# A four-layer graph network on one core: Elu of two attention layers one tick later, and the third layer's sum split over two ticks

## The chip, the cores and the metric

The kernel runs on one core of one Trainium2 chip. The metric is device time in microseconds. Before the change the median of three runs is 7264.87 us (7262.79 to 7265.74).

## What is computed

50,000 nodes with 256 features each pass four blocks; every block is `x = layernorm(x + block(x))`. Block 1 is a hypergraph convolution, block 2 two graph attention layers, block 3 a graph convolution with batch norm, block 4 two more attention layers. 25,000 edges are sorted by target. The change touches block 2 and the first layer of block 4. One attention layer, cut to what matters:

```python
h = (x @ W).reshape(n, HEADS, HID)
e = leaky_relu(a_s[src] + a_d[dst], 0.2)         # self loops are among the edges
ex = exp(e - segment_max(e, dst)[dst])
alpha = ex / segment_sum(ex, dst)[dst]
out = segment_sum(h[src] * alpha[:, :, None], dst).reshape(n, 256) + b
# block 2: elu(out) after each of its two layers, then x = layernorm(x + out)
# block 4, first layer: relu(layernorm(out) * g + b), then W2
```

## The kernel before, in words

The kernel is a row of phases, each with its own buffers and an end at which all engines meet. `layer_phase` (L2465) runs five of them: `l1` (kind `l1a`, first attention layer of block 2), `l2` (`l1b`, second one, with residual and layernorm), `l3` (`gcn`), and, behind a batch-norm phase, `l5` (`l3a`, first attention layer of block 4) and `l6` (`l3b`). The change acts in l1, l2 and l5.

Nodes are permuted so that 25,088 slots (region 0) can have edges that end in them, and as many (region 1) have none. A tile is 128 partitions by 4 rows (J = 4) of one region, so there are 49 tiles of each region, 98 in all. `ORDER` mixes them by hand: in every 11 ticks there are six tiles of region 0 and five of region 1.

A phase is a loop over ticks. In a tick every engine runs its program for that tick, in its own order, and engines are held together only by semaphores. `L` (L2004 to L2012) gives each stage of a tile its tick: a tile with index u in `ORDER` has stage s in tick u + L[s]. Before the change:

- `load` 6: SP loads the tile's rows into ring buffer `a` (L2092), once the tile that held the buffer before is done with. In l2 and l5 that is waiting for `s_z`, which ACT raises when it has normalized that tile (L2244). `resid` loads the residual rows (L2098), `store` stores the result (L2105 in l2, L2113 in l1 and l5). SP takes them in the order batch store L1691, load, resid, store.
- `pre` 8: for region 0 only. ACT scales two of the four rows by the self loop's share (`own_rows`, L2279, eight instructions, the first thing in ACT's tick). DVE (`sum_up`, L2325) scales the edge sums into `part` (L2345), scales the other two rows (L2349), waits for ACT's rows, and adds (L2354), which raises `s_sum`.
- l1 and l2: in tick 9 ACT takes exp of the tile into one of two buffers `ee` (L2257, the last thing in ACT's tick), and in tick 10 (`body`) DVE makes Elu of it (L2373). In l1 this raises `s_u`; in l2 the residual add (L2383) does, and four row statistics (L2399) follow.
- l5: region 1 has its body in tick 8 (four instructions L2390, then the statistics L2399); for region 0, `sum_up` goes on in the same tick with the bias add (L2364) and the statistics.
- With a norm: variance on DVE per pair of tiles (L2408, L2414) one tick after the body, the power -0.5 on POOL (L2131), the shift on DVE (L2421), the norm on ACT five ticks after the body (L2244). l1 and l5 end with transposes (`turn`, PE L2187), their copy (`zt`, ACT L2227 or L2224), the product (PE L2166), and its eviction (DVE L2434 in l1, ACT L2214 in l5).

`Edges` interleaves the edge work: 25 batches of 8 columns, each with POOL gathers (L1667), logits on DVE (L1824 to L1844), their exp on ACT (L1733), weighting and running sums on DVE (L1865, L1881), a copy on ACT that needs the end of the batch (L1737), and shares (L1897 to L1923). DVE's program of a tick is not one part after another: `take_turns` (L114) takes one instruction from each part in turn, edge parts first, then eviction, shift, variance, body, sum.

ACT's order in a tick is own rows, edge work, eviction, `zt`, norm, exp for Elu. So an edge step that comes at the end of DVE's tick (L1733, L1737) holds the `zt`, norm and exp queued behind it.

The ring of `a` has `last - L["load"] + 2` buffers: 7 in l1, 11 in l2, 9 in l5.

Of the kernel before, what the change touches and what calls it, by code (L numbers as in the profile page):

```python
# [7 lines left out]
ALU = mybir.AluOpType  # L8
# [6 lines left out]
D = 256  # L15
# [110 lines left out]
def spread(ap, k):  # L126
    return ap.unsqueeze(len(ap.shape)).to_broadcast([*ap.shape, k])


def over_columns(row, k):  # L130
    return row.unsqueeze(1).to_broadcast([row.shape[0], k, row.shape[1]])
# [1861 lines left out]
class Nodes:  # L1993


    def __init__(self, nc, S, s, kind, edges, rows, rw, resid=None, weight=None, out=None, heads=4, self_act=0):
# [5 lines left out]
        self.mat = kind in ("l1a", "l3a", "gcn")  # L2002
        pre = self.edges.first - SPOT[0] + (4 if self.gat else 2)
        L = self.L = {"pre": pre, "load": pre - 2}  # L2004
        body = L["body"] = pre + 2 if self.elu else pre
        L["resid"] = max(body - 2, 0)
        if self.norm:
            L["var"], L["norm"] = body + 1, body + 5
        L["turn"] = (L["norm"] if self.norm else body) + 1
        L["zt"], L["prod"], L["evict"], L["store"] = (L["turn"] + k for k in (1, 2, 3, 4))  # L2010
        if not self.mat:
            L["store"] = L["norm"] + 1  # L2012
        last = L["norm"] if self.norm else L["turn"]
        self.ra = last - L["load"] + 2
        self.a = [s.sb(f"a{b}", [P, J, rw]) for b in range(self.ra)]
        self.s_in = s.sems("rows_loaded", self.ra)
        if resid is not None:
# [265 lines left out]
    def vector(self, dve, tick):  # L2283
        parts = []
        if tick == 0:
            self.prepare(dve)
        if self.gcn:
            now = self.tile(tick, "store")
            if now:
                parts.append(self.batch_stats(dve, *now))  # L2290
            now = self.tile(tick, "pre")
            if now and now[1] == 0:
                parts.append(self.add_neighbours(dve, *now))
            return parts
        now = self.tile(tick, "evict") if self.kind == "l1a" else None
        if now:
            parts.append(self.evict(dve, *now))
        if self.norm:
            q = self.pair(tick, "var", 3)
            if q is not None:  # L2300
                parts.append(self.shifts(dve, q))
            q = self.pair(tick, "var")
            if q is not None:
                parts.append(self.variance(dve, q))
        now = self.tile(tick, "body")
        if now and (self.elu or now[1]):
            parts.append(self.body(dve, *now))
        now = self.tile(tick, "pre")
        if now and now[1] == 0:
            parts.append(self.sum_up(dve, *now))  # L2310
        return parts
# [13 lines left out]
    def sum_up(self, dve, u, region, t):  # L2325
        H, lk, e = self.heads, self.sum_lk, self.edges
        hw, b, k0 = D // H, t // 2, t % 2 * J
        sh, a = e.share[b % 2], self.a[u % self.ra]
        run = e.run[b % e.nrun][:, k0:k0 + J, 0:D]
        by_head = lambda x: x.rearrange("p j (h c) -> p j h c", h=H)  # L2330
        dve.wait_ge(e.s_nw, b + 1)
        dve.wait_ge(self.s_in[u % self.ra], self.loaded(u))
        sa = self.self_act
        if H == 1:
            dve.wait_ge(self.s_self, t + 1)
            for j in range(J):
                last = dve.scalar_tensor_tensor(a[:, j, 0:D], run[:, j, :], sh[:, 1, k0 + j, 0:1], a[:, j, 0:D], ALU.mult, ALU.add)  # L2337
                if j < J - 1:
                    yield
            last.then_inc(self.s_sum, 1)  # L2340
        else:
            part = self.part[t % 2]
            if t >= 2:
                dve.wait_ge(self.s_sum, t - 1)
            lk.link(dve.tensor_tensor(by_head(part[:]), by_head(run), spread(sh[:, 1, k0:k0 + J, :], hw), ALU.mult))  # L2345
            yield
            if sa < J:
                own = by_head(a[:, sa:J, 0:D])
                lk.link(dve.tensor_tensor(own, own, spread(sh[:, 0, k0 + sa:k0 + J, :], hw), ALU.mult))  # L2349
                yield  # L2350
            lk.settle(dve)
            if sa:
                dve.wait_ge(self.s_self, t + 1)
            dve.tensor_tensor(a[:, :, 0:D], a[:, :, 0:D], part[:], ALU.add).then_inc(self.s_sum, 1)  # L2354
        if self.elu:
            return
        yield
        dve.wait_ge(self.s_sum, t + 1)
        if self.kind == "l3a":
            other = over_columns(self.S["r_L3_gnn_b1"][:], J)  # L2360
        else:
            dve.wait_ge(self.s_rin[u % self.rr], 16 * (u // self.rr + 1))
            other = self.r[u % self.rr][:, :, 0:D]
        dve.tensor_tensor(a[:, :, 0:D], a[:, :, 0:D], other, ALU.add).then_inc(self.s_u, 1)  # L2364
        yield
        dve.wait_ge(self.s_u, u + 1)
        yield from self.row_stats(dve, u)
# [252 lines left out]
```

## Time and profile before

| | us |
|---|---|
| median of three runs | 7264.87 |
| lowest, highest | 7262.79, 7265.74 |
| the profiled execution's own time | 7259.0 |
| its span | 7257.3 |
| phase l1, from its start to the next phase's | about 2832 to 3552 |
| phase l2 | about 3552 to 4404 |
| phase l5 | about 5533 to 6330 |

The profiled execution is 5.9 us below the median. PE is TensorE (PEld its weight loads), DVE VectorE, ACT ScalarE, POOL GpSimd, SP the engine that issues most transfers (SPq its queue). In a row of the timeline or of a line, the number in brackets is the time that the engine stood idle ahead of the instruction, and what ended it. Times in the timeline count from the start of the span; names of tensors have their phase number left out, so `l_a` is `a` in whichever layer phase runs at that time.

### The profile page before, as it was taken

The page shows a single profiled execution, that of the slowest core. Times are in us where ns is not written, and L with a number is a line of the kernel's source. Part 1 is how long each engine was busy: PE and PEld are TensorE (multiplying, and loading weights), DVE is VectorE, ACT ScalarE, POOL GpSimd, SP SyncE. Part 2 cuts the span into 40 slices and gives each one's busy share as a digit, 9 for nine tenths or more (in the row PEclk, how much of TensorE's full clock was granted, in tenths as well). Part 3 has the DMA queues.
Part 4 walks back from the last instruction along what each step waited for, and adds up shares of the span by engine and source line. Part 5 has one row for each costly group of instructions (what it writes and reads, how often), then busy time and mean ns, then how long its engine had stood idle before and what let it go on. Part 6 is the DMA issues. An engine that isn't in the chain of part 4 may idle for free. (4 is left out here: it accounts for less than half of the span.)

```text
span 7257.3 us, 77301 instructions
## 1 busy us (share of the span) xinstructions
PE 3818.6 (53%) x18205; PEld 3002.3 (41%) x18205; DVE 4910.7 (68%) x15616; ACT 3204.3 (44%) x7082; POOL 3988.0 (55%) x3216
## 2 busy tenths in 40 slices
PE   3578880088866884777400005988884666700000
PEld 1267760077755663555400003547773555600000
DVE  6544555545548875999698886866666888676664
ACT  0023330033324552444255555758884777633333
POOL 4767776667766877342244425621114444178887
PEclk9689995599998997999755557999997888855555
DMA  8745447845448996676577767989995666476665
GB/s 307 273 92 77 77 64 272 328 69 78 77 56 318 350 348 212 234 245 235 186 260 260 249 244 286 380 302 327 334 336 188 215 219 211 163 265 226 226 227 188
DMA packets 646102, 1633.93 MB, mean 225 GB/s; under 512 B 128454, under 2 KB 283878, under 8 KB 630290
## 3 DMA queue, kind: packets, MB, share of 16 engines
q1 hardware_dynamic: 459954, 1234.83, 48.9%
q0 software_dynamic: 185696, 394.18, 20.3%
q8 instruction: 150, 2.46, 0.1%
q14 instruction: 302, 2.47, 0.1%
HBM read 816.50 MB, written 813.62 MB: 225 GB/s over the span
## 5 line engine op out<-in xcount | busy, mean ns | idle before, releaser
L1708 PE MATMUL l_pb<-l_jx,k_ones 128*128 128x128 f32 x26 | 6.1, 399 | 1595.9 <-DVE l_jx L1941 1595.9
L802 POOL DMA_INDIRECT NS<-e_tot,e_idx x392 | 647.9, 1653 | 283.3 <-ACT e_tot L1060 210.8
L2244 ACT ACTIVATE l_z<-l_a,l_nb,l_rs 128x256 f32<-128x256 f32 x1176 | 609.7, 598 | 392.7 <-DMA out_dram<-l_z,k_ids 389.9
L1667 POOL DMA_INDIRECT l_eg<-HBT,k_nsrc x392 | 508.2, 1296 | 384.8 <-DVEq L1886 145.0
L1708 PEld LDWEIGHTS l_pb<-l_jx,k_ones 128*128 128x128 f32 x26 | 5.0, 284 | 1596.6 <-DVE l_jx L1941 1596.6
L936 DVE TENSOR_SCALAR e_eq<-e_pk,z_skey 128x128 f32<-128x128 f32 x588 | 204.1, 347 | 621.7 <-DMA NS<-e_tot,e_idx 590.4
L2131 POOL TENSOR_TENSOR l_rs<-l_ve,k_minus_half 128x8 f32<-128x8 f32 x147 | 259.7, 1767 | 533.9 <-DVE l_ve L2414 241.3
L2166 PE MATMUL l_pm<-k_w_L3b,l_zt 128*128 128x258 f32 x1568 | 406.8, 419 | 218.8 <-ACT l_o L2214 214.5
L2138 POOL DMA_INDIRECT out_dram<-l_z,k_ids x392 | 422.1, 1077 | 119.5 <-issue 109.0
L1203 POOL DMA_INDIRECT XH<-n_o,z_home x392 | 399.7, 1020 | 119.2 <-issue 112.4
L2279 ACT ACTIVATE l_a<-l_a,l_eshare 128x64 f32<-128x64 f32 (+1 forms) x1372 | 378.9, 360 | 186.2 <-DVE l_eshare L1923 144.0
L2166 PE MATMUL l_pm<-k_w_L1b,l_zt 128*128 128x264 f32 x1568 | 400.3, 403 | 113.2 <-DVE l_o L2434 109.0
L1060 ACT ACTIVATE e_tot<-e_pa 128x520 f32<-128x520 f32 x196 | 118.3, 604 | 744.2 <-DMA NS<-e_tot,e_idx 731.9
L2399 DVE BATCH_NORM_STATS2 l_bs<-l_a 128x6 f32<-128x256 f32 x1176 | 444.8, 410 | 2.1
L2166 PEld LDWEIGHTS l_pm<-k_w_L3b,l_zt 128*128 128x128 f32 x1568 | 323.3, 212 | 279.1 <-issue 228.2
L1881 DVE SCALAR_TENSOR_TENSOR l_erun<-l_erun,k_same,l_eg 128x260 f32<-128x260 f32 (+2 forms) x880 | 419.7, 477 | 4.0
L1667 POOL DMA_INDIRECT l_eg<-XH,k_psrc x196 | 242.5, 1237 | 323.0 <-DVEq L1886 262.9
L1227 PE MATMUL n_pm<-z_w_L1a,n_zt 128*128 128x264 f32 x1568 | 399.3, 412 | 12.0 <-DVE n_o L1265 11.4
L1011 PE MATMUL e_po<-z_w_e2n,e_hid 128*128 128x256 f32 x1584 | 379.2, 383 | 19.0 <-DVEq L899 19.0
L1020 PE MATMUL e_pr<-e_zt,z_w_n2e 128*128 128x256 f32 x1584 | 379.3, 383 | 0.4 <-issue 0.3
L1420 POOL TENSOR_TENSOR n_rs<-n_ve,k_minus_half 128x8 f32<-128x8 f32 x49 | 80.2, 1636 | 536.7 <-DVE n_ve L1539 536.7
L2166 PEld LDWEIGHTS l_pm<-k_w_L1b,l_zt 128*128 128x128 f32 x1568 | 293.2, 196 | 194.2 <-DVE l_o L2434 114.4
(384 smaller groups left out, 13063.6 us busy)
## 6 DMA issues: line engine op xcount, KB each, us to landing
NS<-z_zero SPq DMA_DIRECT2D x200, 520.0 KB
HBT<-l_o SPq DMA_DIRECT2D x196, 528.0 KB
l_a<-HBT SPq DMA_DIRECT2D x196, 528.0 KB, 9.2
GSUMS<-l_erun SPq DMA_DIRECT2D x72, 1056.0 KB, 5.0
l_a<-XH SPq DMA_DIRECT2D x98, 528.0 KB
HA<-n_o SPq DMA_DIRECT2D x98, 528.0 KB, 7.9
l_a<-HA SPq DMA_DIRECT2D x98, 528.0 KB
n_r<-NS SPq DMA_DIRECT2D x98, 520.0 KB
```

What stands on the lines that cost most here:

```text
L802: pool.indirect_dma_start(out=nodes, out_offset=bass.IndirectOffsetOnAxis(ap=idx[q % DEEP][:, k:k + 1], axis=0), in_=tot[q % 2][:, k, :], ...
L1011: mm = pe.matmul(po[:, k, :], hid[q % 2][:, i, k * P:(k + 1) * P], w2[:, i, 0:D], start=i == 0, stop=i == KC - 1)
L1020: mm = pe.matmul(pr[:, n, :], w1[:, i, n * P:(n + 1) * P], zt[q % 2][:, i].rearrange("p j n -> p (j n)"), start=i == 0, stop=i == KC - 1)
L1203: pool.indirect_dma_start(out=T["XH"], out_offset=bass.IndirectOffsetOnAxis(ap=S["home32"][:, col:col + 1], axis=0), in_=o[t % RO][:, j, : ...
L1227: last = pe.matmul(pm[h][:, i, 0:RW], zt[t % 2][:, k, h * (J // 2) + i, :], weight[:, k, :], start=k == 0, stop=k == KC - 1)
L1667: pool.indirect_dma_start(out=self.g[b % self.ng][:, k, :], out_offset=None, in_=self.table, in_offset=bass.IndirectOffsetOnAxis(ap=self.i ...
L1881: lk.link(dve.scalar_tensor_tensor(rt[:, k, 0:n], before, S["same"][:, b * BC + k:b * BC + k + 1], g[:, k, 0:n], ALU.mult, ALU.add))
L2138: pool.indirect_dma_start(out=self.out, out_offset=bass.IndirectOffsetOnAxis(ap=S["ids32"][:, col:col + 1], axis=0), in_=self.z[u % self.r ...
L2166: last = pe.matmul(self.pm[h][:, i, 0:self.wc], zt[:, k, h * (J // 2) + i, :], self.weight[:, k, 0:self.wc], start=k == 0, stop=k == KC - 1)
L2244: last = act.activation(z[:, j, 0:D], a[:, j, 0:D], ACT.Identity, bias=self.nb[b][:, col:col + 1], scale=self.rs[b][:, col:col + 1])
L2279: last = act.activation(a[:, j, f], a[:, j, f], ACT.Copy, scale=sh[:, 0, t % 2 * J + j, h:h + 1])
L2399: self.stat_lk.link(dve.bn_stats(bs[:, u % 2 * J + j, :], a[:, j, 0:D]))
```

## The change

Elu (`body`) of l1 and l2 comes in tick 11 instead of 10; all stages that are counted from it follow one tick later (resid, variance, norm, turn, zt, prod, evict, store). The exp on ACT stays in tick 9, and there are still two `ee` buffers, so that the exp of tile u now waits for a body (of tile u - 2) of the same tick, not of the tick before. The ring of `a` grows from 7 to 8 buffers in l1 and stays at 11 in l2, where a tile now holds its buffer one tick longer. In l5 `sum_up` ends after its two multiplications in tick 8, and a new part `join_parts` in tick 9 does the add, the bias add and the statistics; region 1's body moves to tick 9 as well, with all later stages one tick later; the ring grows from 9 to 10. No instruction is added or dropped. Phases l3 and l6 are as before.

```diff
--- before.py
+++ after.py
@@ -2002,16 +2002,20 @@
         self.mat = kind in ("l1a", "l3a", "gcn")
         pre = self.edges.first - SPOT[0] + (4 if self.gat else 2)
         L = self.L = {"pre": pre, "load": pre - 2}
-        body = L["body"] = pre + 2 if self.elu else pre
+        body = L["body"] = pre + 3 if self.elu else pre
+        self.split = kind == "l3a"
+        if self.split:
+            body = L["body"] = L["join"] = pre + 1
         L["resid"] = max(body - 2, 0)
         if self.norm:
-            L["var"], L["norm"] = body + 1, body + 5
+            stats = L.get("join", body)
+            L["var"], L["norm"] = stats + 1, stats + 5
         L["turn"] = (L["norm"] if self.norm else body) + 1
         L["zt"], L["prod"], L["evict"], L["store"] = (L["turn"] + k for k in (1, 2, 3, 4))
         if not self.mat:
             L["store"] = L["norm"] + 1
         last = L["norm"] if self.norm else L["turn"]
-        self.ra = last - L["load"] + 2
+        self.ra = last - L["load"] + (1 if kind == "l1b" else 2)
         self.a = [s.sb(f"a{b}", [P, J, rw]) for b in range(self.ra)]
         self.s_in = s.sems("rows_loaded", self.ra)
         if resid is not None:
@@ -2305,6 +2309,9 @@
         now = self.tile(tick, "body")
         if now and (self.elu or now[1]):
             parts.append(self.body(dve, *now))
+        now = self.tile(tick, "join") if self.split else None
+        if now and now[1] == 0:
+            parts.append(self.join_parts(dve, *now))
         now = self.tile(tick, "pre")
         if now and now[1] == 0:
             parts.append(self.sum_up(dve, *now))
@@ -2348,13 +2355,28 @@
                 own = by_head(a[:, sa:J, 0:D])
                 lk.link(dve.tensor_tensor(own, own, spread(sh[:, 0, k0 + sa:k0 + J, :], hw), ALU.mult))
                 yield
-            lk.settle(dve)
-            if sa:
-                dve.wait_ge(self.s_self, t + 1)
-            dve.tensor_tensor(a[:, :, 0:D], a[:, :, 0:D], part[:], ALU.add).then_inc(self.s_sum, 1)
+            if self.split:
+                return
+            yield from self.add_parts(dve, u, t)
         if self.elu:
             return
         yield
+        yield from self.rest_of_sum(dve, u, t)
+
+    def add_parts(self, dve, u, t):
+        a, lk = self.a[u % self.ra], self.sum_lk
+        lk.settle(dve)
+        if self.self_act:
+            dve.wait_ge(self.s_self, t + 1)
+        dve.tensor_tensor(a[:, :, 0:D], a[:, :, 0:D], self.part[t % 2][:], ALU.add).then_inc(self.s_sum, 1)
+        yield
+
+    def join_parts(self, dve, u, region, t):
+        yield from self.add_parts(dve, u, t)
+        yield from self.rest_of_sum(dve, u, t)
+
+    def rest_of_sum(self, dve, u, t):
+        a = self.a[u % self.ra]
         dve.wait_ge(self.s_sum, t + 1)
         if self.kind == "l3a":
             other = over_columns(self.S["r_L3_gnn_b1"][:], J)
```

## Rows read from the trace of the kernel before

**Rows 1.** The page's first line, whole kernel
```profile
span 7257.3 us, 77301 instructions
```
**Rows 2.** Windows, one row a phase: length; busy us (count) of PE, PEld, DVE, ACT, POOL; PEclk, DMA, GB/s
```profile
2832.00:3555.00 723.00, 491.99 (x2384) 391.64 (x2384) 605.28 (x1259) 317.76 (x788) 245.04 (x199) 0.92 0.67 222
3555.00:4396.00 841.00, 6.77 (x28) 5.99 (x28) 741.00 (x2037) 422.15 (x1080) 365.48 (x245) 0.50 0.71 248
5530.00:6328.00 798.00, 489.84 (x2382) 418.49 (x2382) 650.11 (x1994) 542.15 (x1376) 338.58 (x246) 0.82 0.59 200
```
**Rows 3.** Waits of DVE in phase l1 (total us, times, longest us)
```profile
DVE l_a L2373 <- ACT l_ee L2257: 46.1, 37, 1.7
```
**Rows 4.** Waits of DVE in phase l2
```profile
DVE l_a L2373 <- ACT l_ee L2257: 79.4, 33, 3.0
```
**Rows 5.** Waits of DVE in phase l5
```profile
DVE l_a L2354 <- ACT l_a L2279: 89.8, 24, 5.7
```
**Rows 6.** Windows of the three phases without their first and last stretches
```profile
2890.00:3515.00 625.00, 458.84 (x2215) 363.24 (x2216) 553.50 (x1157) 300.62 (x747) 204.99 (x165) 0.96 0.69 235
3600.00:4345.00 745.00, 5.25 (x22) 4.56 (x22) 664.38 (x1823) 378.98 (x979) 320.28 (x210) 0.50 0.72 251
5600.00:6263.00 663.00, 432.59 (x2074) 368.26 (x2075) 571.68 (x1766) 481.42 (x1233) 279.84 (x200) 0.84 0.62 209
```
**Rows 7.** Waits of DVE in the last 65 us of phase l5
```profile
DVE l_a L2354 <- ACT l_a L2279: 5.7, 1, 5.7
```
**Rows 8.** Timeline of l1, one tick: start us, us, engine, line, operation
```profile
3140.61 2.01 ACT L2279 ACTIVATE l_a<-l_a,l_eshare 128x64 f32<-128x64 f32 x8
3140.76 1.23 DVE L2373 SCALAR_TENSOR_TENSOR l_a<-l_ee,l_a 128x1024 f32<-128x1024 f32 x1 [0.87 <-ACT l_ee L2257]
...
3145.69 1.23 DVE L2354 TENSOR_TENSOR l_a<-l_a,l_part 128x1024 f32<-128x1024 f32 x1
```
**Rows 9.** Timeline of l2, one tick with own rows behind a late end of batch
```profile
3971.20 0.26 ACT L1737 ACTIVATE l_erun<-l_em 128x32 f32<-128x32 f32 x1 [9.70 <-DVEq L1886]
...
3974.95 1.66 POOL L2131 TENSOR_TENSOR l_rs<-l_ve,k_minus_half 128x8 f32<-128x8 f32 x1 [0.69 <-ACT l_z L2244]
...
3975.72 2.00 ACT L2279 ACTIVATE l_a<-l_a,l_eshare 128x64 f32<-128x64 f32 x8
3975.84 1.23 DVE L2373 SCALAR_TENSOR_TENSOR l_a<-l_ee,l_a 128x1024 f32<-128x1024 f32 x1 [3.01 <-ACT l_ee L2257]
...
3980.37 1.21 DVE L2354 TENSOR_TENSOR l_a<-l_a,l_part 128x1024 f32<-128x1024 f32 x1
```
**Rows 10.** Row loads of l2: timeline around one load, and the landing times (line L2092)
```profile
3939.20 0.43 SPq L2092 DMA_DIRECT2D l_a<-HBT  x1
...
3942.15 0.32 SPq L2105 DMA_DIRECT2D X<-l_z  x1
...
3955.96 2.02 ACT L2279 ACTIVATE l_a<-l_a,l_eshare 128x64 f32<-128x64 f32 x8 [3.06 <-DVE l_eshare L1923]
...
DMA to landing us min/median/max: 5.5/9.5/10.1
```
**Rows 11.** Timeline of l5: one add that waits, and the body work of another tile
```profile
5918.47 0.68 DVE L2349 TENSOR_TENSOR l_a<-l_a,l_eshare 128x512 f32<-128x512 f32 x1
...
5921.64 2.02 ACT L2279 ACTIVATE l_a<-l_a,l_eshare 128x64 f32<-128x64 f32 x8
...
5923.76 1.28 DVE L2354 TENSOR_TENSOR l_a<-l_a,l_part 128x1024 f32<-128x1024 f32 x1 [4.61 <-ACT l_a L2279]
...
5926.33 1.41 DVE L2399 BATCH_NORM_STATS2 l_bs<-l_a 128x6 f32<-128x256 f32 x4
...
5928.31 1.64 DVE L2390 SCALAR_TENSOR_TENSOR l_a<-l_a,k_loop,k_r_L_gnn_b 128x256 f32<-128x256 f32 x4
```
**Rows 12.** Timeline of the end of l1: ACT, two ticks in a row
```profile
3533.13 1.08 ACT L2227 ACTIVATE l_zt<-l_pt 128x512 f32<-128x512 f32 x2 [3.35 <-PE l_pt L2187]
...
3537.57 1.08 ACT L2227 ACTIVATE l_zt<-l_pt 128x512 f32<-128x512 f32 x2 [3.35 <-PE l_pt L2187]
```

## Prediction, made before the changed kernel was run

> **What bounds the kernel now.** I read the page for the span [rows 1], then cut the trace into phases by the first and last instruction of each and asked for windows of the three that the change touches [rows 2]. They take 723, 841 and 798 us, a third of the span. In each, DVE is the busiest engine: 605, 741 and 650 us; ACT has 318, 422 and 542. So I asked next what DVE waits for. In l1 the largest entry is Elu waiting for ACT's exp, 46.1 us in 37 waits of at most 1.7 us [rows 3]. In l2 it is the same line, 79.4 us in 33 waits, up to 3.0 us [rows 4]. In l5 it is the add of the parts, waiting for ACT's own rows: 89.8 us in 24 waits [rows 5].
>
> The test of whether these waits set the time is whether DVE has any other idle time. It has nearly none [rows 6]: in the middle of l2 745 us hold 664.4 us of DVE work, 80.6 us are left, and the Elu waits are 79.4 less what lies outside the window. In the middle of l5, 663 less 571.7 leaves 91.3, against 89.8 less the 5.7 at its end. In the middle of l1, 625 less 553.5 leaves 71.5, of which 46.1 is Elu and the rest waits for PE and short gaps. DVE therefore works through its program without a break but for these waits, and a wait taken off DVE comes off the phase, unless another takes its place.
>
> Why the waits are there: ACT's program of a tick is released by something that DVE does at the end of its tick (the batch copy at 3971.20, after ACT had stood idle for 9.70 us [rows 9]). ACT then has norm and exp to do while DVE is already at the next tick's Elu. In l5 the own rows are behind eviction, zt and norm in the same way: they begin at 5921.64, while DVE had both its products by 5918.47 + 0.68 = 5919.15 and stood for 4.61 us [rows 11].
>
> **l1, Elu a tick later.** The exp that Elu needs now is from ACT's tick before last, so its 46.1 us of waits go. What is late next? The own rows stand behind the exp in ACT's queue, and the add needs them. In the tick shown they end at 3140.61 + 2.01 = 3142.62, and the add starts at 3145.69 [rows 8]; with the wait of 0.87 us gone it would start at 3144.82, still 2.2 us after. So no wait replaces it there. The new wait of the exp for the body of its own tick costs ACT nothing that counts: in l1 Elu is in the first round of DVE's tick, and ACT is the engine that is late. What moves with Elu (turn, zt, prod, evict, store: PE's transposes and products, ACT's copies, DVE's evictions, SP's store) keeps its order and its distance; the buffers grow with it, so SP's load is held no longer than now. Some waits lie where PE would hold the short tick instead; the lower bound of that cost is 0, the upper is the whole 46.1, and I take 3 us, since the unexplained idle time in the window is small. One more tick is drained at the end. There a tick is 4.44 us (3533.13 to 3537.57 [rows 12]), set by PE, and DVE saves in exchange an Elu of 1.23 us and two evictions at the start: between 0 and 4.4 us, I take 2. Gain 46.1 - 3 - 2 = 41.1.
>
> **l2, Elu a tick later.** 79.4 us of waits go. The dangerous tick is the one shown [rows 9], which has the late batch end and own rows in a row: Elu would start at 3975.84 - 3.01 = 3972.83, the add at 3980.37 - 3.01 = 3977.36, and the own rows end at 3975.72 + 2.00 = 3977.72. So 0.4 us of the 3.0 comes back, in one tick of 11; 9 times 0.4, about 4 us. The nearest bounds are 0 and the 3.0 us of the wait itself, 27 us. The residual load moves a tick later with its use. The exp now waits for the residual add of its tick (second round on DVE); behind it on ACT is only the next tick's own rows, which DVE needs a full tick's work later: 0.
>
> Row loads are tighter in l2, as the ring stays at 11. A load is now released by the norm of ACT's tick just before, not by the one before that. For the tile whose own rows run at 3955.96, the load went out at 3939.20; now it leaves with the store at 3942.15, and lands a median of 9.5 and at most 10.1 us later [rows 10], at 3951.7 to 3952.3. Its user moves forward by the 3.0 us wait that is gone, to 3952.96. So it is in time by about 1 us in the tightest place; the other tiles have more. Upper bound: 9 places, late by the 2 us that contention might add, 18 us; lower 0. I take 0, since that is what the landing rows give. SP holds the residual load and a store behind the load, which have the same or a later need. The end costs up to one tick's leftover, 1 us taken. Gain 79.4 - 4 - 1 = 74.4.
>
> **l5, the split.** Both products stay in tick 8; the add goes to the first round of tick 9, a whole ACT block later. In the tick shown [rows 11] DVE goes on at 5919.15 with a region 1 body (1.64) and statistics (1.41), to 5922.2, and takes about 1 us of edge steps ahead of the join in the next tick, against own rows that end at 5921.64 + 2.02 = 5923.66. So 0.5 of 4.6 us stays, in about one of three waits: 8 times 0.5, 4 us (bounds: 0 and half of all, 45). The wait of 5.7 us at the end [rows 7] is no gain, as ACT is working without a break there and sets the end. The bias add, statistics and all later stages move with their buffers. The later `s_sum` is waited for by shares and running sums of batches whose tiles were added several ticks before: 0. The spread of work also evens DVE's ticks (before, a region 0 tile had sum and statistics in one tick), which helps a little; 0 taken, and up to 10 us over the three phases for the range. The extra tick at the end is ACT-bound: 2 us, as in l1. Gain 89.8 - 5.7 - 4 - 2 = 78.1.
>
> **Sum.** 41.1 + 74.4 + 78.1 = 193.6 us. Against the profiled execution's own time, 7259.0 - 193.6 = 7065.4; the median of the runs stands 5.9 us above that execution, which gives 7071. POOL, DMA and PE all have to do the same work in less time (DMA's busy share is 0.59 to 0.71 [rows 2]), and I set 4 us aside for that: 7075.
>
> **A rule weighed.** In l2 POOL's power runs from 3974.95 for 1.66 us, and the Elu that starts within it, at 3975.84, takes 1.23 us, no longer than elsewhere [rows 8, 9]. DVE is not held up by it. The Trainium skill says otherwise (SBUF — State Buffer, "SBUF: two separate sides"): a Vector instruction with two SBUF inputs and a GpSimd one that reads SBUF exclude each other for a whole instruction. By that rule DVE, now at work where it stood idle, would be stopped behind the power, and the sum would shrink as in the third rival below; by the row it stays.
>
> **Rivals.** *The waits slide on.* ACT is still released at the end of DVE's tick, so its lateness could fall on the next consumer: own rows for the add in l2, shares and join in l5. For it: 9.70 us of ACT idle ahead of each release [rows 9]. Against it: the slack of 2.2 us in l1 and the 0.4 us in l2. If half of the 215.3 us of waits comes back, the gain is about 100: 7165.
>
> *Slower: l2's ring becomes the loop.* A buffer's load, own rows and norm now have three ticks between two norms. Own rows are 2.0 us, and edge steps, norm and exp together at most the 4.5 us between 3971.20 and 3975.72 [rows 9]; three ticks are about 24 us, at 8 us a tick (841 us for 98 tiles and both ends [rows 2]). So the loop decides once a load takes over 24 - 6.5 = 17.5 us to land, and the kernel is slower than before only if l2 also loses the 119 us gained elsewhere, at a tick of 9.2 us and a landing of 21 us. At 25 us, for one, a tick would be 10.5 us and l2 245 us longer than before: 7265 - 119 + 245 = 7391. Landings of 5.5 to 10.1 us [rows 10] speak against it.
>
> *Each POOL power stops DVE once.* 98 powers in l2 and l5 (49 each) at the 1.66 us of rows 9 are 163 us that come back: 7238. This is the time that the skill's lock would give; the unhindered Elu speaks against it.
>
> *The change does not do what it says:* the join still waits as before because ACT is the bound of l5. ACT has 481 us in 663 [rows 6], so it is not; the time would be 7075 + 78 = 7153, inside the first rival's spread.
>
> **How the numbers follow.** Forecast, 7045 to 7110: 0.80. Slide, 7110 to 7210: 0.14. Stopped by POOL, 7238: 0.02. No gain, within 0.2% (14.5 us, about what a measurement of this kernel can tell from no change): 0.02. Ring, 7391: 0.02. The low end is all 215 us and some of the 10 us of evening out: 7265 - 215 = 7050. The high end takes in the upper bounds that are most open (27 in l2 for own rows, 18 for loads, 30 of l5's) on top of the sum: 7150. Faster 0.96, same 0.02, slower 0.02.
>
> **What would show it.** L2373's wait for exp is gone from DVE's list in l1 and l2. L2354 waits for own rows under 10 us in l5 and about 4 in l2, and 0 in l1. The windows shrink to about 682, 767 and 720 us, with DVE's busy time unchanged, so a share of 0.88 to 0.97. ACT's waits for DVE shrink by the same amounts. SP's load in l2 directly follows the norm of the tick before. I am wrong if DVE L2345 or ACT L2279 wait for the load of `l_a` by tens of us, if DVE waits appear on PE in l1, or if the DVE instructions themselves grow longer.

## The result and the profile after

The kernel after takes 7084.99 us (median of five runs, 7071.34 to 7096.27), the kernel before 7264.87 us (7250.31 to 7266.57): a ratio of 0.9748, 95% interval 0.9728 to 0.9768. The forecast was 7075 with a range of 7050 to 7150. The profiled execution is the longest of the five, 7096.27 us; its span stands beside the 7257.3 of [rows 1]:

```profile
span 7094.5 us, 77303 instructions
```

To read it by phase I cut both traces at the memset of `l_erun` with which each attention layer's edge part begins on DVE (line 1773); l3 and the batch norm are cut at their own first instruction on DVE. Every phase then has an exact length, and it shows at once which part of a difference belongs to the change:

| | ahead of l1 | l1 | l2 | l3 | batch norm | l5 | l6 |
|---|---|---|---|---|---|---|---|
| before | 2833.0 | 720.3 | 851.5 | 466.9 | 662.7 | 794.8 | 928.2 |
| after | 2848.1 | 688.9 | 772.8 | 472.4 | 664.6 | 718.8 | 929.0 |

The three touched phases gain 31.4, 78.7 and 76.0 us, 186 in all; the untouched ones are 23 us longer in this execution, 15 of it ahead of l1, where no instruction differs. Hence the 163 us between the spans. The lines of the code stand lower than before: Elu L2373 is now L2395, its exp L2257 is L2261, the add L2354 is L2371, own rows L2279 are L2283, the eviction L2434 is L2456 (its first part L2432 is L2454), the product L2166 is L2170.

Windows of l1, l2, l5, and of the middle of each, columns as in [rows 2]:

```profile
2847.00:3537.00 690.00, 493.72 (x2384) 394.26 (x2384) 601.09 (x1259) 319.03 (x788) 237.71 (x198) 0.91 0.70 232
3537.00:4309.00 772.00, 6.77 (x28) 5.99 (x28) 740.12 (x2037) 424.20 (x1082) 370.29 (x246) 0.50 0.78 272
5447.00:6165.00 718.00, 489.78 (x2381) 417.18 (x2381) 645.92 (x1990) 540.84 (x1376) 344.94 (x246) 0.86 0.65 222
2905.00:3500.00 595.00, 462.32 (x2226) 367.20 (x2225) 550.67 (x1156) 304.04 (x752) 197.59 (x164) 0.95 0.71 246
3585.00:4250.00 665.00, 6.59 (x28) 5.89 (x28) 660.05 (x1820) 374.45 (x966) 320.93 (x209) 0.50 0.80 278
5515.00:6105.00 590.00, 438.69 (x2107) 372.39 (x2108) 573.51 (x1792) 485.10 (x1244) 284.21 (x201) 0.89 0.70 237
```

DVE's work in each phase is what it was, within 5 us of [rows 2], in less time. In the middle of l2 it now fills 660 of 665 us and in that of l5 573.5 of 590, where [rows 6] had 80 and 91 us left over. In l1 44 of 595 us are still open. The waits say what is in them. Those of DVE that bear on the change are, in l1:

```profile
DVE l_o L2456 <- PE l_pm L2170: 35.5, 20, 2.7
DVE k_asd L2454 <- PE l_pm L2170: 10.8, 9, 3.3
```

in l2:

```profile
DVE l_a L2371 <- ACT l_a L2283: 1.8, 4, 0.4
```

and in l5, where they are its two longest:

```profile
DVE l_nb L2443 <- POOL l_rs L2135: 9.7, 2, 8.5
DVE l_a L2371 <- ACT l_a L2283: 8.9, 11, 2.6
```

The wait of Elu for its exp [rows 3, 4] is in neither list, and the 89.8 us of [rows 5] have become 8.9. What l1 has instead is the eviction waiting for the product: 46.3 us, where the kernel before had 26.9 on the same two lines:

```profile
DVE l_o L2434 <- PE l_pm L2166: 20.3, 12, 2.8
DVE k_asd L2432 <- PE l_pm L2166: 6.6, 6, 1.6
```

The change gave back 46.1 us and took 19.4.

Where do those come from? Before, 25.4 of the 26.9 us lay in the last 80 us of the phase, and there the kernel after has 26.9, nearly the same. New are the waits of the middle: six of 2.0 to 2.3 us, 13.1 in sum, one in each eleven ticks of the hand-written order (72 us), one of 2.7 at the start and five of 0.7. The timeline of l1 shows one of the six:

```profile
3158.15 0.26 ACT L1737 ACTIVATE l_erun<-l_em 128x32 f32<-128x32 f32 x1 [5.43 <-DVEq L1886]
...
3158.99 1.06 ACT L2231 ACTIVATE l_zt<-l_pt 128x512 f32<-128x512 f32 x2
...
3159.71 1.06 PE L2191 MATMUL l_pt<-k_ident,l_a 128*128 128x128 f32 x8 [2.19 <-ACT l_zt L2231]
...
3160.61 5.42 PE L2170 MATMUL l_pm<-k_w_L1b,l_zt 128*128 128x264 f32 x16
...
3164.35 0.71 DVE L2456 TENSOR_TENSOR l_o<-l_pm,k_row_b 128x528 f32<-128x528 f32 x1 [2.34 <-PE l_pm L2170]
```

ACT stands 5.43 us for the end of DVE's batch, and its `zt` copy, which doesn't need that batch, stands behind it. PE's transposes want the buffer that this copy frees, the product follows late, and the eviction holds DVE for 2.34 us. It is the same late ACT that held Elu before the change; in l1 it now reaches DVE by way of PE.

ACT got new waits too: its exp now stands for the bodies of its own tick. In l1 and l2, in this order:

```profile
ACT l_ee L2261 <- DVE l_a L2395: 19.6, 20, 1.9
```
```profile
ACT l_ee L2261 <- DVE l_a L2405: 54.7, 29, 6.0
```

Whether they cost anything is an open question at this point.

### The profile page after: what moved, and what is told of

Same layout as the page of the kernel before. It is cut to its first block and busy times, and to the rows that moved or that the text cites. A ratio compares the mean times of both kernels' runs of the same rounds, so it can differ in the third digit from the quotient of the medians.

```text
span 7094.5 us, 77303 instructions
## 1 busy us (share of the span) xinstructions
PE 3822.3 (54%) x18205; PEld 3003.3 (42%) x18205; DVE 4901.1 (69%) x15616; ACT 3205.9 (45%) x7082; POOL 3995.6 (56%) x3216
## 5 line engine op out<-in xcount | busy, mean ns | idle before, releaser
L2135 POOL TENSOR_TENSOR l_rs<-l_ve,k_minus_half 128x8 f32<-128x8 f32 x147 | 279.5, 1901 | 447.6 <-ACT l_z L2248 327.1
L2170 PE MATMUL l_pm<-k_w_L3b,l_zt 128*128 128x258 f32 x1568 | 404.4, 416 | 130.3 <-ACT l_o L2218 115.2
L1203 POOL DMA_INDIRECT XH<-n_o,z_home x392 | 401.3, 1024 | 120.2 <-issue 113.5
L2170 PE MATMUL l_pm<-k_w_L1b,l_zt 128*128 128x264 f32 x1568 | 403.6, 406 | 79.6 <-DVE l_o L2456 76.7
L2283 ACT ACTIVATE l_a<-l_a,l_eshare 128x64 f32<-128x64 f32 (+1 forms) x1372 | 379.6, 365 | 100.1 <-DVE l_eshare L1923 72.5
L2170 PEld LDWEIGHTS l_pm<-k_w_L3b,l_zt 128*128 128x128 f32 x1568 | 321.0, 210 | 191.7 <-issue 141.1
L2170 PEld LDWEIGHTS l_pm<-k_w_L1b,l_zt 128*128 128x128 f32 x1568 | 297.6, 198 | 160.8 <-DVE l_o L2456 74.8
```

Of the source, the lines that this page charges most:

```text
L1203: pool.indirect_dma_start(out=T["XH"], out_offset=bass.IndirectOffsetOnAxis(ap=S["home32"][:, col:col + 1], axis=0), in_=o[t % RO][:, j, : ...
L2170: last = pe.matmul(self.pm[h][:, i, 0:self.wc], zt[:, k, h * (J // 2) + i, :], self.weight[:, k, 0:self.wc], start=k == 0, stop=k == KC - 1)
L2283: last = act.activation(a[:, j, f], a[:, j, f], ACT.Copy, scale=sh[:, 0, t % 2 * J + j, h:h + 1])
```

## The experiments

Twelve kernels were run, on three chips, each beside the kernel before on the same chip: 7272.56 us on the first, 7165.88 on the second, 7186.35 on the third. The two faster chips save most of their time ahead of l1 (2746 to 2770 us there against 2833 to 2850). The touched phases agree between chips: where a kernel leaves them as the kernel after has them, l1 takes 687.0 to 689.2 us and l5 718.5 to 719.3 on all three, and l2 771.7 to 772.8 on the first and the third (no run of the second has it so). So phases are compared across chips, and totals only by their ratio. `half_prod_l1`, `ring10`, `ring12` and `ee3` were run once each, the others four or five times; their phases come from one profiled execution each.

**Each part alone** (first chip). `l1_only` keeps Elu's delay for l1 alone, `l2_only` for l2, `split_only` has the split of l5 and no delay:

```diff
-        body = L["body"] = pre + 3 if self.elu else pre
-        self.split = kind == "l3a"
+        body = L["body"] = pre + (3 if kind == "l1a" else 2) if self.elu else pre
+        self.split = False
```

These are the lines of `l1_only`. `l2_only` has "l1b" in place of "l1a", `split_only` puts 2 in place of 3 and keeps the split. The ring of l2 has 11 buffers in all three, as before and after.

> Only phase l1 has its Elu a tick later; l2 and l5 are as before. My theory (DVE's waits are what is gained, and they add up phase by phase): phase l1 shrinks from 720 us by the 31 us that it shrank in the full change, l2 and l5 stay within 3 us of 852 and 795, the whole kernel is 7265 - 31 = about 7234. Elu's wait for exp is 0 in l1 and still near 79 us in l2; DVE waits for PE in l1 by about 46 us instead of 27. Rival (the parts help each other, for instance by the DMA traffic or the larger buffers): l1 gains a different amount by more than 5 us, or l2 or l5 move.

> Only phase l2 has its Elu a tick later, with its ring of 11 buffers; l1 and l5 are as before. My theory: l2 shrinks from 852 us by 79, to about 773; l1 stays at 720 and l5 at 795, the kernel at about 7186. Rival (part of the gain in l2 is a consequence of l1's change): l2 gains less than 74.

> Only the sum of l5 is split; l1 and l2 are as before. My theory: l5 shrinks from 795 us by 76, to about 719, the kernel to about 7189; the add waits for own rows by about 9 us instead of 90. The three single gains (31, 79, 76) add up to the full change's 186 within 5 us. Rival (parts overlap): the sum of the three is off by more than 10 us.

| | us | ratio to before | the phase, before to now |
|---|---|---|---|
| `l1_only` | 7245.44 | 0.9960 (0.9946 to 0.9975) | l1 720.3 to 687.0 |
| `l2_only` | 7188.32 | 0.9887 (0.9870 to 0.9903) | l2 851.5 to 771.7 |
| `split_only` | 7191.00 | 0.9890 (0.9873 to 0.9906) | l5 794.8 to 719.1 |

Each part moves its own phase, and the other two by at most 2 us: 33.3, 79.8 and 75.7 us, together 188.8 against the 186 of the whole change. The parts add up, as phases with an end at which all engines meet should let them. The waits on PE in l1 come with l1's part alone:

```profile
DVE l_o L2456 <- PE l_pm L2170: 35.6, 20, 2.7
DVE k_asd L2454 <- PE l_pm L2170: 8.9, 8, 2.1
```

and in `split_only` the add of l5 waits as in the kernel after:

```profile
DVE l_a L2371 <- ACT l_a L2283: 8.8, 11, 2.6
```

**Is it PE that holds l1?** `half_prod_l1` is the kernel after without half of the product's matmuls in l1.

```diff
-                        for k in range(KC):
+                        for k in range(1 if self.kind == "l1a" else KC):
```

> The changed kernel, but phase l1's product takes only the first 128 of the 256 input features, so half of its matmuls (784 of 1568) are left out, and its output is another. Theory for the 10 us that l1 fell short of the forecast: once DVE no longer waits for exp it waits for PE's products, 46 us in l1 instead of 27, so l1 is in part bound by PE. Then l1 shrinks from 689 us by the 46 us of DVE's waits for PE at most, to 645 to 655, most of it in the last 15 ticks, and in the middle (2905 to 3500 before) DVE's 32 us of waits go below 5. Rival (the evictions wait for DVE's own order or for ACT's copy of the transposed rows, which has the same length): l1 stays above 675.

```profile
2840.00:3503.00 663.00, 381.02 (x1600) 285.38 (x1600) 600.76 (x1258) 317.92 (x788) 241.64 (x198) 0.78 0.72 242
```
```profile
DVE l_o L2456 <- PE l_pm L2170: 13.9, 15, 1.6
DVE k_asd L2454 <- PE l_pm L2170: 3.2, 3, 1.5
```

l1 comes to 662.3 us, 26.6 less than in the kernel after, and the two waits to 17.1, which is 29.2 less. So what l1 lost is time in which DVE waited for the product. It doesn't reach the 645 to 655 us expected; 17.1 us of waits remain. Seven of them, 8.1 us in sum, still come once in eleven ticks, and the one at 3081.46 ends the same chain as above: ACT stands 5.42 us for the end of the batch, `zt` follows, PE's transposes have waited 3.08 us for it, and the eviction waits 1.24 us for what is left of the product. The matmuls also lost less time than their number says: 784 fewer, at 1.95 us for eight (the product at 3152.28 in the kernel after), would be 191 us, and PE's busy time fell by 113. The 784 transposes, of which none was left out, took 132.2 us in place of 107.0. The mean granted clock of the window, between the levels 0.5 (1.2 GHz) and 1.0 (2.4 GHz), is 0.78, where the kernel after had 0.91 with PE busy for 494 us. The single run took 7050.61 us in all.

**Is it the order in which ACT takes its work?** `before_edges_last` is the kernel before, with none of the change. It swaps two lines, so that ACT does its eviction, `zt`, norm and exp ahead of the edge steps that wait for the end of DVE's batch. `edges_last` is the kernel after with the same swap. The swap acts in all five layer phases. Both ran on the second chip.

```diff
                     nodes.own_rows(act, tick)
+                    nodes.scalar(act, tick)
                     edges.scalar(act, tick)
-                    nodes.scalar(act, tick)
```

> The kernel before, with no stage moved; only ACT's program of a tick in the five layer phases has the edge steps last, behind zt, norm and exp, and not ahead of them. My theory of the cause is that ACT is late because an edge step that waits for the end of DVE's tick (L1733, L1737) stands ahead of exp and own rows. Then this edit removes the same waits as the change, from the other side: Elu's wait for exp and the add's wait for own rows fall below 20 us each in their phases, l1 is about 675 us, l2 about 773, l5 about 720, and the kernel is at 7060 to 7100. Rival (ACT has simply too much to do in these ticks, whatever its order): less than half of the 215 us of waits goes and the kernel stays above 7150. A second rival (the edge steps come too late for DVE's shares, L1913, and weights, L1865): new waits there of more than 50 us.

> The changed kernel with the same edit of ACT's order. In l1 of the changed kernel one eviction in each 11 ticks waits 2.2 us for PE, whose transposes had waited for an ACT copy (zt) that stood behind the end of a batch. My theory: with the copy ahead of the edge steps these waits go in the middle of l1, about 20 us, l1 is at 665 to 675, l2 stays at 773, l5 falls by some 5 us as the add's 9 us of waits go; the kernel is 20 to 30 us below the changed one. Rival (PE's product is the limit, not the copy): l1 stays at 689.

`before_edges_last` takes 6964.40 us, a ratio of 0.9719 (0.9703 to 0.9736); `edges_last` 6958.93 us, 0.9710 (0.9694 to 0.9726). The windows of l1, l2 and l5 of `before_edges_last`:

```profile
2750.00:3421.00 671.00, 483.67 (x2384) 388.57 (x2384) 599.56 (x1258) 318.26 (x788) 241.86 (x198) 0.93 0.72 239
3421.00:4192.00 771.00, 6.77 (x28) 5.99 (x28) 739.32 (x2037) 424.21 (x1082) 381.38 (x246) 0.50 0.78 273
5315.00:6034.00 719.00, 488.46 (x2384) 416.89 (x2384) 648.41 (x1993) 541.72 (x1376) 340.08 (x246) 0.86 0.62 222
```

and DVE's waits there in l1, then in l5:

```profile
DVE l_o L2434 <- PE l_pm L2166: 19.3, 12, 2.8
DVE k_asd L2432 <- PE l_pm L2166: 5.2, 4, 1.6
```
```profile
DVE l_a L2354 <- ACT l_a L2279: 5.6, 5, 4.1
```

Elu's wait for the exp is gone from l1 and l2, with Elu where it always was. The second rival did not come about: DVE's waits for shares and weights stay under 2 us in each of the three phases. In l3 and l6, which the swap also reorders, it gains nothing that shows: 458.7 and 925.1 us, where `ring10` on the same chip, without it, has 461.5 and 924.5. The total that I had expected, 7060 to 7100, was reckoned for the first chip; the ratio gives 7061 there. This settles the cause. The waits of [rows 3, 4, 5] were not for want of a tick; they were ACT's queue, in which work that was ready stood behind work that wasn't. The swap alone gives l2 and l5 what the change gives them (771.5 and 718.7 against 772.8 and 718.8) and gives l1 more (671.4 against 688.9). With the swap in place, the change adds nothing that these runs can tell: the two intervals overlap, and by phase it is +1.3 in l1, +1.2 in l2 and -3.9 in l5. `edges_last` (l1 672.7, l2 772.7, l5 714.8, all three as expected) also shows the route through PE closed to the level of before, in l1:

```profile
DVE l_o L2456 <- PE l_pm L2170: 19.0, 12, 2.0
DVE k_asd L2454 <- PE l_pm L2170: 7.8, 5, 3.1
```

**How much slack have the own rows?** `own4` (second chip) is the kernel after with ACT scaling all four rows of a tile and not two (`self_act=4` for 2 in the three calls of `layer_phase`). It takes 27 or 28 us of work off DVE in each phase (from 601, 740 and 646 us of the kernel after).

> The changed kernel with ACT scaling all four rows by the self share in l1, l2 and l5 (own rows of two to four), so that DVE's multiplication of the other two (L2356, 49 of 0.68 us a phase, 33 us) is gone and ACT has 49 times 2.0 us, 98 us, more. Theory that DVE's work is now the bound of all three phases: l1 loses 15 to 33 us, l2 about 15 (its add had only 0.4 us to spare and own rows end 2 us later), l5 5 to 33, since the split gives own rows a tick more; the kernel is at 7000 to 7050. Rival (with the waits gone ACT is as near to its limit as DVE, above all in l5 with 541 us in 718): l5 grows, and the kernel is not faster.

It takes 7015.33 us, 0.9786 (0.9770 to 0.9802), with l1 at 683.6 us (5 under the kernel after), l2 at 780.3 (7.5 over) and l5 at 752.6 (34 over). The waits of the add in l1, l2 and l5:

```profile
DVE l_a L2371 <- ACT l_a L2283: 26.6, 18, 2.9
DVE l_a L2371 <- ACT l_a L2283: 37.0, 23, 3.4
DVE l_a L2371 <- ACT l_a L2283: 68.4, 35, 4.9
```

I had expected gains in all three phases; the gain in l1 is a third of the least that I had named, l2 grew, and in l5 the rival was right. What DVE is spared comes back as waiting: the slack for own rows that the change found in l1 and l2 is smaller than the two more rows take.

**Is the ring of l2 long enough?** The change leaves it at 11 buffers with a tile in it for one tick longer. `ring10` (second chip) has one fewer, `ring12` (third chip) one more: 12 (its expectation, which also says so, calls that two more by mistake).

```diff
-        self.ra = last - L["load"] + (1 if kind == "l1b" else 2)
+        self.ra = last - L["load"] + (0 if kind == "l1b" else 2)
```

> The changed kernel with 10 instead of 11 buffers of rows in l2, so that a load is released by the norm of its own ACT tick, two ticks ahead of its use and not three. Forecast by the same reckoning as in the prediction: the tightest load now leaves with the norm one tick later still, some 5 to 8 us, and lands about 9.5 us after that, so that DVE L2352 or ACT L2283 wait for the load by 3 to 6 us in one or two of 11 ticks: l2 grows from 773 by 20 to 100 us. It shows how far the ring of the changed kernel is from its limit. Rival (the ring has more slack than reckoned): l2 grows by less than 10 us.

> The kernel after with two more slots than it has in the ring of the second layer (12 against 11 as ring10 had 10). If the ring as the change leaves it is long enough for the loads, l2 stays at 770-774 us and the waits for own rows of the load stay near 2 us as they are; if the change had made the ring a limit, l2 falls by over 5 us, in the same way as it rose by 14.7 us with one slot fewer.

`ring10` takes 6996.17 us with l2 at 787.5, so 14.7 us longer than with 11, less than the 20 to 100 expected and more than the rival's 10. ACT then waits for the loads, and, which I had not reckoned with, more for the store:

```profile
ACT l_z L2245 <- DMA X<-l_z: 74.6, 36, 4.2
ACT l_a L2283 <- DMA l_a<-HBT: 29.0, 20, 5.8
```

In the kernel after the own rows' wait for a load is a single one of 5.8 us, at the start of the phase. `ring12` takes 7002.27 us with l2 at 772.1: 0.7 less than with 11 buffers, which is as much as the same phase differs from kernel to kernel. Eleven are enough, with less than one buffer's slack, and ten cost 15 us.

**What does ACT's new wait cost?** `ee3` (third chip) is the kernel after with a third `ee` buffer.

```diff
-            self.ee = [s.sb(f"ee{b}", [P, J, D]) for b in range(2)]
+            self.ee = [s.sb(f"ee{b}", [P, J, D]) for b in range(3)]
 ...
-                if u >= 2:
-                    act.wait_ge(self.s_u, u - 1)
+                if u >= 3:
+                    act.wait_ge(self.s_u, u - 2)
 ...
```

> The kernel after with three buffers for the exponentials instead of two in the attention layers. ACT's exp no longer stands for the DVE's Elu of a later tick, so the waits ACT L2261 has for the DVE (19.6 us in l1, 54.7 us in l2 in the kernel after) shrink. If DVE is the engine that sets the length of l2, as I hold, l2 stays at 770-775 us and l1 at 685-692 us in spite of this. The rival: ACT's new wait is what kept l1 from its full forecast gain; then l1 comes to about 677-680 us.

It takes 6994.19 us. The waits of 19.6 and 54.7 us on `s_u` have become, in l1 and l2:

```profile
ACT l_ee L2261 <- DVE l_a L2371: 0.2, 1, 0.2
```
```profile
ACT l_ee L2261 <- DVE l_a L2371: 1.3, 1, 1.3
```

and the phases stay: l1 686.9, l2 772.9. 74 us of ACT's waiting were worth 2 us at most, in one run, because ACT was not the engine that was short.

**Can more of DVE's work go to ACT once ACT isn't held up?** `edges_last_own4` and `edges_last_own3` (third chip) are `edges_last` with four or three of the four rows on ACT.

> The kernel after, with ACT's steps between the batches put last in a tick and with all four rows of the share with the own rows on ACT. If ACT was late with the own rows in own4 only because it began its tick late behind those steps, then now the DVE's waits for the own rows stay small (under 10 us in each attention layer where own4 had 26.6, 37.0 and 68.4), DVE has about 33 us (l1), 30 us (l2), 30 us (l5) less to do than in the kernel after, and l1 comes to 645-660 us, l2 to 742-755, l5 to 690-705: 6880-6915 us against the 6959 of edges_last. The rival: four rows of about 0.3 us each are simply too late for the add whatever comes ahead of them; then the waits stay at 25, 35 and 60 us and the time is 6970-7020 us, no better than edges_last.

> As edges_last_own4 with one row fewer on ACT. If the share with the own rows has a balance between the engines, this lies between edges_last and edges_last_own4 where the latter gains (some 6920-6940 us), and under both where the latter loses (about 6945 us, since three rows end some 0.3 us a tick earlier than four).

| rows on ACT, with the swap | l1 | l2 | l5 | us | ratio to before |
|---|---|---|---|---|---|
| 2 (`edges_last`, second chip) | 672.7 | 772.7 | 714.8 | 6958.93 | 0.9710 (0.9694 to 0.9726) |
| 3 | 662.1 | 760.3 | 714.7 | 6950.34 | 0.9669 (0.9652 to 0.9686) |
| 4 | 656.4 | 748.0 | 746.1 | 6970.37 | 0.9702 (0.9686 to 0.9719) |

In l1 and l2 it comes out as I expected: with ACT's tick no longer beginning late, four rows are in time. The add's waits of `edges_last_own4` in l1, l2 and l5 are, against 26.6, 37.0 and 68.4 in `own4` (a row costs ACT about 0.9 us, since its work in l1 goes from 319 to 409 us for 98 rows more; the 0.3 us of the two expectations is near that of one of the row's four instructions):

```profile
DVE l_a L2371 <- ACT l_a L2283: 7.8, 11, 2.4
DVE l_a L2371 <- ACT l_a L2283: 3.8, 6, 2.4
DVE l_a L2371 <- ACT l_a L2283: 16.4, 12, 3.5
```

In l5 I was wrong by some 50 us: 746.1 where I had expected 690 to 705, and with it in the total, 6970.37 against 6880 to 6915. A wait that I had named as a rival for `before_edges_last` but not here, and the windows of the middle and the end of the phase, show why:

```profile
DVE l_eden L1913 <- ACT l_eex L1741: 38.1, 21, 3.2
```
```profile
5353.00:5918.00 565.00, 417.05 (x1895) 350.93 (x1896) 510.96 (x1601) 527.92 (x1513) 269.53 (x196) 0.87 0.66 231
5918.00:6031.00 113.00, 92.84 (x489) 81.44 (x487) 48.31 (x186) 88.02 (x194) 12.84 (x8) 0.92 0.39 147
```

ACT has 528 us of work in a middle of 565, more than DVE's 511, since it evicts l5's product as well. DVE's two waits for it, 54.5 us in sum, are more than the 26 us of work that DVE is spared against `edges_last`. By these figures ACT has become the bound there. With three rows l5 is level with `edges_last`, and `edges_last_own3` is the fastest version of this study: 3.3% under the kernel before, against 2.5% for the change. Four rows in l1 and l2 with three in l5 would by the table take 5.7 and 12.3 us off it, an estimate of 6932 us on that chip; that version was not run.

## Why the prediction was right, point by point

| term | forecast | measured |
|---|---|---|
| l1, gain | 41.1 | 31.4 (33.3 alone) |
| l2, gain | 74.4 | 78.7 (79.8 alone) |
| l5, gain | 78.1 | 76.0 (75.7 alone) |
| sum | 193.6 | 186 (188.8) |

- **The test for the bound held.** DVE's idle time in the middle of each phase was nearly all in the waits to be removed, so I took a microsecond off DVE for one off the phase. In l2 and l5 that is what happened, within 4.3 and 2.1 us.
- **l1: the mis-sized term is PE.** The mechanism was right and this size was not. The step "the lower bound of that cost is 0, the upper is the whole 46.1, and I take 3 us, since the unexplained idle time in the window is small" chose too low. DVE's waits for the product grew by 19.4 us. The idle time that already existed said how much PE cost while Elu's waits gave it room, not what it would cost without them. `half_prod_l1` shows that the waits on PE are what is left, and `edges_last` that l1 is 16.2 us shorter once the `zt` copy ahead of PE no longer stands behind the edge steps. The order was in the front part of this document: `zt` stands behind the edge steps just as exp does. I followed that for the exp only. That l1 fell 10 us short and not 16 has other reasons that the trace shows in part: nothing is seen of the 2 us set aside for the extra tick (the waits on PE in the last 80 us grew by 1.5 us, which the 19.4 hold), DVE's own work in the phase is 2.6 us less (603.5 to 600.9), and its other waits are 2.2 us less.
- **l2: own rows 4 us, measured 1.8; loads 0, measured 0.** Of the 79.4 us none is left, and DVE's work is 2.5 us less (742.7 to 740.2). The one tick that I had worked out with 0.4 us is in the list with 0.4 us as its longest. `ring12` bears out the 0 for the loads, and `ring10` shows how near the edge it was. No row gave the 2 us that contention might add to a load, an upper bound; the row loads of l2 took 5.3 to 10.1 us after (median 7.2), where they had taken 5.5 to 12.2 (9.2), so nothing was added.
- **The exp's new wait, taken as 0.** I said so for l1 and for l2; 74 us of it appeared and `ee3` shows that they cost at most 2.
- **l5: 4 us left of the add's wait; measured 8.9.** The end of the phase had two waits, 5.7 us for own rows [rows 7] and 5.5 for POOL's power; now it has 2.6, and 1.2 and 8.5 for the power, so 12.3 in place of 11.2. I had counted no gain there, which was right. The forecast is 2.1 us off because errors cancel: the add's waits gave back 80.9 us, but those for POOL grew by 4.2 and one for a transfer (L1941) by 3.3.
- **POOL, DMA and PE in less time, 4 us set aside.** POOL's power did grow longer; no phase can be shown to pay for it. The other 23 us of the profiled execution lie in phases that the change doesn't touch. With them that execution is 27 us over the 7069 that the same sum gives for it. The median of the runs stands 11 us under that execution, and so 10 us over the forecast: the medians differ by 179.9 us where 189.9 was forecast. 7.5 of these 10 us are the three phases'. The runs of each kernel spread over 16 to 25 us, so that a total this close is in part luck.
- **The signs named beforehand.** DVE's share of the three phases is 0.87, 0.96 and 0.90. ACT's waits for DVE shrink by 81 us in l2 (the sum of its list goes from 428 to 347) and by 27 in l1 (341 to 314). One of the conditions for being wrong, waits of DVE on PE in l1, came true in part, and it is where the error is.

**The rivals.** *The waits slide on* was right in kind in l1, where 19.4 us came back by way of PE and not of the own rows; in l2 and l5 10.7 us of 169.2 came back. *The ring becomes the loop* is out: even ten buffers cost 14.7 us. *Each power stops DVE once* is out, below. *The join waits as before because ACT is the bound of l5* is out for this change, and came true in part once two more rows went to ACT (68.4 us of the add's waits in `own4`).

What the prediction lacked is a question: not only "what does this wait cost?" but "why is the producer late?". It names the cause (ACT released by the end of DVE's tick) and prices a way around it; two swapped lines remove it and are worth as much or more.

## What to carry to other kernels

When a consumer waits for a producer that itself was idle shortly before, look at what stood at the head of the producer's queue. If a step that waits for a late signal has independent work behind it, reorder that queue first. Another tick of delay also took the wait away in l2 and l5, but it costs buffers, and in l1 it moved 19.4 of 46.1 us to the next consumer. And when waits are taken off the busiest engine, follow everything else that stands behind the same late step: its next consumer is where the remainder shows up. Moving work to another engine is then a question of that engine's own load phase by phase, as the three and four rows show.

## What the runs showed of the hardware that I had not expected

POOL's power takes longer in the kernel after, while DVE is not held up. The row of the page after:

```profile
L2135 POOL TENSOR_TENSOR l_rs<-l_ve,k_minus_half 128x8 f32<-128x8 f32 x147 | 279.5, 1901 | 447.6 <-ACT l_z L2248 327.1
```

It was 1767 ns in the kernel before. In l2, where DVE is busiest, the mean went from 1662 to 1980 ns, and in the same phase the 98 Elus of DVE took 1203 ns each, against 1214 before. The mean hides two kinds. The longest power of l2 is this one:

```profile
4060.55 1.23 DVE L2395 SCALAR_TENSOR_TENSOR l_a<-l_ee,l_a 128x1024 f32<-128x1024 f32 x1
4061.09 4.61 POOL L2135 TENSOR_TENSOR l_rs<-l_ve,k_minus_half 128x8 f32<-128x8 f32 x1 [0.49 <-ACT l_z L2248]
4061.69 1.23 DVE L2352 TENSOR_TENSOR l_part<-l_erun,l_eshare 128x1024 f32<-128x1024 f32 x1
...
4062.93 1.23 DVE L1865 TENSOR_TENSOR l_eg<-l_eg 128x1024 f32<-128x1024 f32 x1
...
4064.16 1.21 DVE L2405 TENSOR_TENSOR l_a<-l_a,l_r 128x1024 f32<-128x1024 f32 x1
```

It begins while DVE is at an Elu, which reads two tensors. Sorted so over the whole trace after, 66 of the 147 powers begin while DVE has an instruction with two tensor inputs (TENSOR_TENSOR or SCALAR_TENSOR_TENSOR) under way; they take 2186 ns in the mean, and 28 of them more than 2 us. The other 81 take 1.63 to 1.74 us. In the trace before, 38 begin so and 13 of these take more than 2 us, and the other 109 take 1.63 to 1.69. So the mean grew mostly because more powers begin beside such an instruction, and a single one can grow by 3 us.

The prediction weighed the rule of the Trainium skill (SBUF — State Buffer, "SBUF: two separate sides") that a Vector instruction with two SBUF inputs and a GpSimd one that reads SBUF exclude each other for a whole instruction. What POOL does agrees with it: the 4.61 us hold the rest of the Elu and three whole instructions of DVE after it. DVE's side doesn't show here: of its TENSOR_TENSOR over 1024 elements, the 61 that begin within a power take 1216 ns in the mean, and the others 1214. The spans on POOL are rough, and no run varied this by itself.

The phases ahead of l1, without a changed instruction, differ by some 80 us between the first chip and the other two. POOL's scatters of line 802 take the same 1.65 us each on both; POOL waits there for ACT 210.8 us in the trace of the kernel before and 166.2 us in `before_edges_last` on the second. Why was not found.
